# Second attention of an eight-layer kernel: TensorE's key features of slices 2 and 3 ahead of the turns of the last batch's queries, and VectorE's masked copy of the sums ahead of a batch's first maximum

## The reference, cut to what matters

```python
def favorplus_features(x, proj, eps=1e-6):
    xw = einsum('bhtd,hmd->bhtm', x, proj)
    xw = xw - max(xw, axis=-1, keepdims=True)
    return exp(xw) * exp(-0.5 * sum(x * x, axis=-1, keepdims=True)) + eps
phiQ, phiK = features(Q * scale) / sqrt(m), features(K * scale) / sqrt(m)
KV = einsum('bhtm,bhtd->bhmd', phiK, V)
Ksum = sum(phiK, axis=2)
out = einsum('bhtm,bhmd->bhtd', phiQ, KV) / (einsum('bhtm,bhm->bht', phiQ, Ksum)[..., None] + EPS)
x = x + merge(out) @ Wo.T + bo
```

## Time and profile before

| what | value |
|---|---|
| median of 3 runs | 1058.72 us (1055.12 to 1060.01) |
| profiled execution, its own time | 1050.42 us |
| span of the profiled execution | 1048.6 us |
| TensorE busy | 920.4 us, 88% |
| VectorE busy | 776.2 us, 74% |
| ScalarE busy | 409.8 us, 39% |
| GpSimd busy | 349.1 us, 33% |
| mean granted clock of TensorE | 0.947 |
| chain that ended last | TensorE 57%, VectorE 33% |

### The profile page before, as it was taken

How to read it: one execution, slowest core, us unless ns; L and a number is a source line. 1 busy time by engine, 2 the same in 40 slices (tenths; PEclk the granted TensorE clock), 3 DMA queues, 4 the chain that set the end, 5 groups by cost and what they waited for, 6 DMA issues and landing times.

```text
span 1048.6 us, 16651 instructions
## 1 busy us (share of the span) xinstructions
PE 920.4 (88%) x6134; PEld 525.5 (50%) x6156; DVE 776.2 (74%) x1837; ACT 409.8 (39%) x678; POOL 349.1 (33%) x446
## 2 busy tenths in 40 slices
PE   7889999999999978889999985798999888988686
PEld 3434444443443555553534441555657456767454
DVE  5678888767667477787586579757665997788984
ACT  2435556554324344343433357132231334332232
POOL 6372323222213353322333320322121344343333
PEclk9899999999999998889999997699999899998887
DMA  5362122211000000000000000000000000000000
GB/s 135 106 182 78 48 69 60 72 35 72 1 1 1 1 1 1 1 1 1 1 0 1 1 1 0 3 1 1 1 1 2 1 1 1 2 2 3 0 11 30
DMA packets 11532, 24.34 MB, mean 23 GB/s; under 512 B 1323, under 2 KB 7635, under 8 KB 11315
## 3 DMA queue, kind: packets, MB, share of 16 engines
q1 hardware_dynamic: 11152, 22.30, 7.3%
q10 hardware_dynamic: 294, 0.91, 0.3%
HBM read 15.69 MB, written 7.34 MB: 22 GB/s over the span
## 4 chain that ended last, share of the span: by engine, by line
PE 57%; DVE 33%; issue 4%; POOL 2%; ACT 2%; DMA 1%; DVEq 0%; SPq 0%; POOLq 0%; ACTq 0%
PE ps L1065 5%; PE ps L1072 4%; PE ps L1060 4%; PE ps L419 3%; PE ps L369 3%; DVE XN L166 2%; PE ps L2122 2%; DVE a_MN L549 2%; PE ps L2119 2%; PE ps L389 2%; DVE g_C L1878 2%; PE ps L2725 2%; PE ps L945 2%; PE ps L1084 1%; PE ps L1045 1%
## 5 line engine op out<-in xcount | busy, mean ns | idle before, releaser
L549 DVE TENSOR_REDUCE a_MN<-ps 128x1 f32<-128x384 f32 (+3 forms) x154 | 93.2, 637 | 24.3 <-PE ps L372 22.7
L1288 POOL TENSOR_TENSOR f_Y<-f_Y,f_TT 128x512 f32<-128x512 f32 x48 | 60.9, 1269 | 131.9 <-DVE f_TT L1144 131.9
L1236 ACT ACTIVATE f_HH<-ps,pack_zero 128x512 f32<-128x512 f32 x64 | 44.0, 687 | 95.9 <-PE ps L1060 95.9
L119 POOL TENSOR_TENSOR rs<-t,mhalf 128x4 f32<-128x4 f32 x36 | 37.1, 1031 | 130.7 <-DVE t L102 129.2
L673 ACT ACTIVATE a_PT<-ps 128x1024 f32<-128x1024 f32 x56 | 57.3, 1024 | 57.4 <-PE ps L389 57.2
L1144 DVE SCALAR_TENSOR_TENSOR f_TT<-ps,pack_zero,f_X 128x512 f32<-128x512 f32 x64 | 47.8, 747 | 33.5 <-PE ps L1072 33.1
L1065 PE MATMUL ps<-f_XS,pack_zero 128*128 128x512 f32 x128 | 72.0, 645 | 0.0
L1072 PE MATMUL ps<-f_HH,pack_zero 128*128 128x512 f32 x128 | 65.8, 595 | 5.0 <-DVE f_TT L1144 5.0
L1060 PE MATMUL ps<-f_XS,pack_zero 128*128 128x512 f32 x128 | 67.3, 607 | 0.7 <-DVE f_XS L1028 0.7
L369 PE MATMUL ps<-a_KS,a_QS 72*128 72x128 bf16 (+3 forms) x224 | 53.8, 303 | 9.0 <-DVE a_MN L549 8.0
L1028 DVE TENSOR_TENSOR f_XS<-ps,XNT 128x512 f32<-128x512 f32 x64 | 43.7, 685 | 17.1 <-PE ps L945 15.0
(11 more groups left out here) (336 smaller groups left out, 2206.0 us busy)
## 6 DMA issues: line engine op xcount, KB each, us to landing
scratch<-a_parts SPq DMA_DIRECT2D x16, 384.0 KB, 3.7
a_QS<-scratch SPq DMA_DIRECT2D x14, 288.0 KB
a_KS<-scratch SPq DMA_DIRECT2D x42, 96.0 KB
pack_one<-in_one SPq DMA_DIRECT2D x1, 2694.5 KB, 9.3
pack_zero<-in_zero SPq DMA_DIRECT2D x3, 884.5 KB, 4.6
X<-in_x SPq DMA_DIRECT2D x4, 256.0 KB, 10.0
out_x<-X SPq DMA_DIRECT2D x4, 256.0 KB, 2.1
a_QS<-a_MT SPq DMA_DIRECT2D x42, 4.0 KB
```

The lines of the kernel that those rows point to most:

```text
L549: dve.tensor_reduce(M.a_MN[:, n % 2, ti, h0:h0 + k], bank(M, M.bank["a_max", n, jj], 128 * (ti + 1) * k).rearrange("p (a c) -> p a c", a=k ...
L1288: pool.tensor_tensor(M.f_Y[:, i, :], M.f_Y[:, i, :], M.f_TT[:, u % 3, :], ALU.add).then_inc(made.sem, made.tick(n, u))
```

## The change

TensorE: the features of key slices 2 and 3 are issued ahead of the turns j = 0 and j = 1 of the queries, and no longer behind them. The fillers move: out go those in bank 4 ahead of the turns (4, 6 and 2 of them in batches 1, 2 and 3) and those in bank 2 ahead of turn 2 (4 in batches 2 and 3); in come 3 in the turn's own bank ahead of turn 0, 2 ahead of turn 2, and 2 in bank 4 ahead of the query features of slices 2 and 3, in batches 1, 2 and 3 each. In all 20 fillers become 21. The new ones of the turns stand behind the wait for the bank. VectorE: the masked copy of the sums is issued ahead of slice 0 and no longer behind slice 1. ScalarE and GpSimd keep their order.

```diff
--- before.py
+++ after.py
@@ -1354,8 +1354,8 @@
         i, made = "kq".index(w), S["p_feat"]
         for g in pair:
             take(pe, M, 2 + g)
-        if b == 0 and w == "k" and pair[0] == 0:
-            filler(pe, M, 2, 2)
+        if (b, w, pair[0]) == (0, "k", 0) or (b and w == "q" and pair[0] == 2):
+            filler(pe, M, 2 + pair[0], 2)
         pe.wait_ge(S["p_qt"].sem, S["p_qt"].at(b, w))
         for j in range(4):
             for g in pair:
@@ -1401,9 +1401,10 @@
         m.then_inc(made.sem, made.tick(b))
         M.freed[bk] = (S["p_kvr"], (b,))
 
-    def queries(b, j):
+    def queries(b, j, fill=0):
         made = S["p_qturn"]
         bk = spare("p_q", b, j)
+        filler(pe, M, bk, fill)
         if j == 0:
             pe.wait_ge(S["p_exp"].sem, S["p_exp"].at(8 * b + 7))
         for g in range(4):
@@ -1433,16 +1434,12 @@
         project(b, "q")
         if b >= 2:
             features_output(pe, S, M, b - 2, spare())
-        if b:
-            filler(pe, M, 4, (0, 4, 6, 2)[b])
-            queries(b - 1, 0)
-            queries(b - 1, 1)
         features(b, "k", (2, 3))
         if b:
+            queries(b - 1, 0, 3)
+            queries(b - 1, 1)
             sums_turned(b - 1)
-            if b >= 2:
-                filler(pe, M, 2, 4)
-            queries(b - 1, 2)
+            queries(b - 1, 2, 2)
             queries(b - 1, 3)
         values(b)
         if b == 2:
@@ -1510,11 +1507,11 @@
         norm_front(dve, S, M, 3, b, M.X)
 
     for b in range(4):
+        if b:
+            sums(b - 1)
         for w in "kq":
             for g in range(4):
                 subtract(b, w, g)
-                if w == "k" and g == 1 and b:
-                    sums(b - 1)
                 if w == "k" and g == 2 and b >= 2:
                     leave(b - 2)
                 if w == "q" and g == 1 and b >= 2:
```

## The result

The changed kernel took 1048.12 us in the median of 8 executions (1045.88 to 1051.8), the kernel before 1056.15 us (1054.6 to 1060.01). The ratio is 0.992, with a 95% interval of 0.9899 to 0.9941: 8.0 us faster, within 6.2 to 10.7. Forecast were 6.4 us and 1052.3 us; of the 4.2 us between that time and the measured one, 2.6 us are the kernel before, whose median had been 1058.72 us. All these executions taken together, 68 of the kernel before have a median of 1055.1 us and 20 of the changed kernel one of 1047.9: 7.2 us.

A forecast was written before the change was run, and what follows sets the result against it. Handovers in the second attention were the bound: TensorE's turns wait for VectorE's masked copy, VectorE for features queued behind those turns. Gains 0.8 + 3.7 + 1.9 = 6.4 us off 1058.72 give 1052.3 us; range 1045.5 to 1059.5.

The forecast's parts named there:

- Batch 1: TensorE-limited stretch of batch 1: idle time removed less added fillers, end set by GpSimd; 0.8 us, bounds 0.4 and 1.9.
- The next term: Batch 1: GpSimd's bias add holds VectorE's addition, sets the end, and comes 0.8 us earlier with TensorE's projection.
- Batch 2: Keys of batch 2: L197 4.2 us earlier, 0.2 lost behind it; 4.0 us, 3.7 after an allowance of 0.3.
- the allowance of 0.3: Batch 2's keys: 0.3 us taken off the 4.0 for VectorE additions held by GpSimd's squares.
- Two signs: Batch 2 in the new trace: clock near 1.0 in the keys; TensorE's wait for L197 still there, 2 us or so.
- Batch 3: Keys of batch 3: slice 2's maximum earlier, its features still at the lower clock; 1.9 us, upper bound 3.6.
- From L197 on, VectorE's own two slices and GpSimd's root set L166: Batch 3 behind L197: VectorE's slices and GpSimd's root set L166, so the fillers there don't count.
- Shifts as a whole: Everything behind L166 and L181, to the feed-forward layer, hangs in one line and moves together; no further gain or loss.
- The clock stays up: Rival: batch 3's lower-clock stretches go, 1.7 us for features and up to 3.5 at the end; 1047.1 us, chance 0.22.
- GpSimd holds VectorE: Rival: batch 2's additions of slices 1 and 2 wait out key copies, 3.0 us together; 1055.3 us, chance 0.18.
- The clock falls on the path: Rival: lower clock in batch 1 and behind L197 of batches 2 and 3 costs 12 us; 1064.3 us, chance 0.06.
- No effect: Rival: something else ends the waits, or the kernel's end absorbs them; 1058.7 us, chance 0.12.

The follow-up runs named there:

- the two half changes: Two runs on the kernel before: TensorE's order and fillers only, 1051.58 us; VectorE's masked copy ahead of slice 0 only, 1050.14 us.
- TensorE's half alone: Kernel before with TensorE's order and fillers of the changed kernel, VectorE's masked copy still behind slice 1: 1051.58 us, ratio 0.9975.

## Why the prediction was right, and which terms were off

The way: the turns' wait for the masked copy, and VectorE's wait behind them, were the path, and reordering closed them. The profiles of the two half changes show it; the times of the whole alone would not.

*Batch 1, 0.8 us forecast, 1.4 measured.* From TensorE's projection of the queries to the maximum of query slice 2 it was 13.37 us (386.65 to 400.02) and is 12.80: 0.57 gained where the sum of gap and fillers said 0.4. TensorE before:

```profile
386.65 1.10 PE L1338 MATMUL ps<-XNT,pack_zero 128*128 128x512 f32 x2
```

The changed kernel, TensorE, GpSimd and VectorE:

```profile
393.66 1.10 PE L1338 MATMUL ps<-XNT,pack_zero 128*128 128x512 f32 x2
...
405.61 1.28 POOL L1653 TENSOR_TENSOR X<-X,pack_zero 128x512 f32<-128x512 f32 x1
...
406.46 0.69 DVE L1481 TENSOR_REDUCE p_MX<-ps 128x16 f32<-128x512 f32 x1 [1.54 <-PE ps L1363]
407.18 0.18 DVE L1486 TENSOR_TENSOR p_MX<-p_MX,p_HF 128x16 f32<-128x16 f32 x1
```

The next term was mis-sized. I let the hold by GpSimd's bias add set the end, and let that add come 0.8 us earlier, with TensorE's projection. It came 1.9 us earlier (13.81 us behind the projection of batch 1's queries before, 11.95 after): its input, ScalarE's copy of the projected keys, stands in ScalarE's queue behind the exponential of query slice 0, and that moved by 1.9 us. So GpSimd ended the add at 406.89, the addition came at 407.18 and took 0.18 us, and the whole hold of 0.87 was gone. It lay within the bound of 1.9.

*Batch 2, 4.0 less 0.3 forecast, 4.0 measured.* From the reciprocal to L197 4.26 us less (forecast 4.2); from there to the query maximum 5.32 us where it was 5.05, 0.27 lost (forecast 0.2); no hold came, so the allowance of 0.3 was not needed. Two signs that I had named failed here. The clock was not near 1.0 but down behind the wait for `p_OT`, and the cover for the features, 1.4 us forecast and 0.9 left (416.4 against 417.33), kept that harmless. And TensorE's wait for L197, "2 us or so", was not there: fillers, features and turns at the lower clock filled the time, and it came to turn 2 just as L197 ended. That the sum held even so is in part luck.

*Batch 3, 1.9 forecast, 1.5 measured.* From the first addition, which waits for the halved squares, to the maximum of slice 2 it is 4.02 us (439.32 to 443.34), and was 6.05: 2.03. An addition there took 0.39 us, not 0.18, under GpSimd. Then the step "From L197 on, VectorE's own two slices and GpSimd's root set L166" failed: from L197 to L166 it is 8.64 us, and was 8.30. The query maximum now came 4.83 us behind L197, not 3.85, so VectorE and not GpSimd's root came last at L166, 0.34 lost. The two fillers are 0.43 of that delay. The rest is the clock: turns 0 and 1 took 1.91 us at its lower level (the row at 444.49), and TensorE came to the fillers of turn 2 0.67 us after L197 had ended, where before it had stood waiting for it. In the run without fillers the maximum came later still, 5.52 us behind L197, with both pairs of turns at the lower clock.

*Sum.* 1.4 + 4.0 + 1.5 = 6.9 us by these distances, which end at L166 of batch 3. "Shifts as a whole" then was a term put at nothing that was not nothing: from L166 to L962 it is 10.57 us and was 11.35, another 0.8 (0.1 and 0.3 against the other two profiles of the kernel before). From the projection of batch 1's queries to L962 that makes 78.4 - 70.7 = 7.7 us. The stretch from batch 0's sums shows only 5.9, and 6.4 against the mean of three, because the clock was down in these sums, ahead of all that moved. So the sum of the forecast has the right size and the right two large terms, but that it meets the 6.4 of the stretch to the tenth is luck. The 5.9, 7.2 and 8.0 us of the timings do not decide between 6.4 and 7.7.

*The rivals.* "The clock stays up" did not come, and its price was off by one term: 1.7 us for the features of batch 3 is right (1.5 with the fillers ahead of the waits), but 3.5 for the end is not. From L181 to L962 it was 8.14 us before and is 7.48 without fillers, with the clock up, but also in the changed kernel, with the clock down at L181: 0.7 us is all there was, and VectorE's two slices, reciprocal, product and copy are the floor. "GpSimd holds VectorE" came in part and small, 0.2 us an addition. "The clock falls on the path" showed its mechanism, not its size: some 1.2 us behind L197 of batch 2 in four profiles (6.50 to 6.62 us to the query maximum), one of them of the kernel before. "No effect" is out.

*The rule against the change.* The Trainium skill, page "SBUF — State Buffer", section "SBUF: two separate sides", says that a VectorE operation with two SBUF inputs and a GpSimd operation that reads SBUF lock each other out for a whole instruction. For GpSimd's bias add and squares, with two inputs of 512 columns, the runs agree: in the run of TensorE's half alone the addition of 0.90 us ended at 418.35, and the squares, started at 417.27 for 1.04 us, at 418.31. For the key copies they do not, as the last section shows, and not for GpSimd's small operation L119 either (two inputs of 4 columns, 1.04 us): an addition 0.12 us into it took 0.18 us (425.56 in the changed kernel).

## What to carry to other kernels

Where two engines hand work back and forth, look at what stands in each queue between the release and the one who waits: here each engine held back, by position alone, an instruction that the other was waiting for, and in the profiles only moving both gave the whole. Read such a change by distances inside its stretch, when the whole scatters by several us: in the two profiles of the changed kernel they repeated to 0.03 us. Compare windows that hold the same work, not the same microseconds, and take more than one profile, since the clock's pattern differs between executions of one kernel. And look for a small instruction that takes several times its usual length: the engine beside it may be what to move.

## What was not expected of the hardware

GpSimd's key copy, one input in SBUF and 1.49 us long, holds a VectorE addition with two SBUF inputs only in its first 0.64 us. GpSimd and VectorE of batch 3 in the changed kernel:

```profile
443.82 1.49 POOL L1636 TENSOR_SCALAR p_PK<-p_XW 128x512 f32<-128x512 f32 x1
447.73 1.49 POOL L1636 TENSOR_SCALAR p_PK<-p_XW 128x512 f32<-128x512 f32 x1 [2.43 <-ACT p_XW L1554]
```

```profile
444.06 0.39 DVE L1486 TENSOR_TENSOR p_MX<-p_MX,p_HF 128x16 f32<-128x16 f32 x1
...
448.00 0.37 DVE L1486 TENSOR_TENSOR p_MX<-p_MX,p_HF 128x16 f32<-128x16 f32 x1
```

Both additions end 0.63 and 0.64 us after the copy's start (444.45 - 443.82 and 448.37 - 447.73). The addition of the earlier trace rows that began 0.55 us into a key copy took 0.17 us. In the twelve profiles, from 370 to 475 us, it is so throughout: 23 additions that began within 0.3 us of a key copy's start ended 0.63 or 0.64 us after it, and those that began 0.49 us or more into one took 0.17 or 0.18 us.

The clock fell where TensorE had hardly stood still. In the changed kernel it had been idle for 1.01 us ahead of 412.36, with 16-column products and one projection before that, and the next work ran at 1.2 GHz (2.05 us). The idle time alone does not decide it: in the run with GpSimd's bias add early, whose TensorE program is that of the changed kernel, the same work behind 1.00 us of idle took 1.13 us, and in the kernel before it took 1.13 us behind 1.87 us of idle. Why it fell in one and not in the other stays open.
